# Moving a graph layer's last combination and normalisation out of a stage of its own into the slices' stage, group by group, with the second layer's sums stored to memory at eviction

## The reference

```python
xn = layernorm(x)
enc = h = xn
for l in range(2):                           # two graph attention layers, 8 heads of 64
    q, k, v = h @ Wq[l] + bq[l], h @ Wk[l] + bk[l], h @ Wv[l] + bv[l]
    a = sum(q[dst] * k[src]) / 8             # per edge and head
    e = exp(a - segment_max(a, dst)[dst])
    agg = segment_sum(e / (segment_sum(e, dst)[dst] + 1e-16) * v[src], dst)
    h = agg + (h @ Ws[l] + bs[l]) + enc
y = layernorm(h) * ln_g + ln_b               # this is the last combination
gnn = layernorm(relu(y @ W1 + b1) @ W2 + b2 + y) * ln_g + ln_b + enc
mid = xn @ W_in + b_in                       # the mixer, 8 heads of 64, 32 slices each
q, k, v = softmax(mid @ Wq, over slices), softmax(mid @ Wk, over nodes), mid @ Wv
mix = (q @ (k.T @ v)) @ W_out + b_out
x = x + gnn + mix
out = x + ffn(layernorm(x))                  # ternary weights
```

## Time and profile before

| | us |
|---|---|
| median of 3 runs (3349.22 to 3351.88) | 3349.69 |
| the profiled execution, by its own clock | 3346.05 |
| its span, first to last instruction | 3344.3 |
| PE / DVE / POOL / ACT busy | 2558.1 / 2347.1 / 1708.9 / 1239.1 |
| last eviction of the second layer's sums begins | 2348.76 |
| first transfer of the slices' stage | 2431.69 |
| first transfer of `node_mlp` | 2610.76 |

### The profile page before, as it was taken

How to read it: one execution, slowest core, us unless ns; L and a number is a source line. 1 busy time by engine, 2 the same in 40 slices (tenths; PEclk the granted TensorE clock), 3 DMA queues, 4 the chain that set the end, 5 groups by cost and what they waited for, 6 DMA issues and landing times. The chain is left out here.

```text
span 3344.3 us, 46214 instructions
## 1 busy us (share of the span) xinstructions
PE 2558.1 (76%) x10373; PEld 1750.8 (52%) x10373; DVE 2347.1 (70%) x4332; ACT 1239.1 (37%) x6570; POOL 1708.9 (51%) x1618
## 2 busy tenths in 40 slices
PE   2888866664988869996666668878077799869998
PEld 1766522222765547872222256655056576657776
DVE  5777687778977767767777798777834346476665
ACT  0344378776000011007777700000233232155554
POOL 0101377777777751117777777777400235344444
PEclk8999998988899999998888879999588899989999
DMA  1544577776777775437777767777130323261111
GB/s 41 182 151 163 175 237 236 239 237 195 204 219 226 228 224 161 133 122 240 236 235 239 229 188 224 223 226 221 55 101 13 126 101 114 73 201 38 38 38 37
DMA packets 228144, 549.19 MB, mean 164 GB/s; under 512 B 32920, under 2 KB 50946, under 8 KB 227918
## 3 DMA queue, kind: packets, MB, share of 16 engines
q0 software_dynamic: 106240, 348.21, 35.4%
q1 hardware_dynamic: 110158, 177.31, 15.8%
q10 hardware_dynamic: 11520, 20.98, 1.8%
HBM read 471.88 MB, written 74.49 MB: 163 GB/s over the span
## 5 line engine op out<-in xcount | busy, mean ns | idle before, releaser
L1189 POOL DMA_INDIRECT edge_ring<-v_rows,edges_src x664 | 655.3, 987 | 202.3 <-issue 160.9
L1352 PE MATMUL edge_psQ<-layer_q_space,layer_y_space 128*128 x1992 | 553.2, 426 | 268.1 <-DVE layer_y_space L1220 266.7
L1189 POOL DMA_INDIRECT edge_ring<-k_rows,edges_src x664 | 628.3, 946 | 252.1 <-issue 141.9
L1389 PE MATMUL edge_psA<-layer_q_space,edge_hot 128*128 128x256 f32 (+1 forms) x2656 | 652.6, 398 | 130.9 <-DVE edge_hot L1284 82.8
L1308 ACT ACTIVATE layer_y_space<-layer_y_space 128x64 f32<-128x64 f32 x2656 | 637.2, 241 | 234.3 <-DVE layer_y_space L1220 233.2
L1389 PEld LDWEIGHTS edge_psA<-layer_q_space,edge_hot 128*128 128x128 f32 x2656 | 491.2, 193 | 292.0 <-issue 224.8
L1295 DVE TENSOR_TENSOR layer_q_space<-edge_ring,edge_psQ 128x512 f32<-128x512 f32 x664 | 456.7, 688 | 149.9 <-DMA edge_ring<-v_rows,edges_src 144.4
L1220 DVE TENSOR_TENSOR layer_y_space<-edge_psQ,edge_ring 128x512 f32<-128x512 f32 x664 | 433.8, 685 | 177.9 <-DMA edge_ring<-k_rows,edges_src 165.0
L1352 PEld LDWEIGHTS edge_psQ<-layer_q_space,layer_y_space 128*128 128x128 bf16 x1992 | 211.0, 106 | 610.4 <-issue 512.5
L103 PE MATMUL proj_psP<-proj_w,proj_xT 128*128 128x512 f32 x1920 | 480.4, 409 | 43.9 <-DVE proj_enc L867 32.3
L1308 ACT ACTIVATION_READ_ACCUMULATOR layer_y_space<-layer_y_space 128x1 f32 x2656 | 494.9, 186 | 0.0
(11 more groups left out here) (287 smaller groups left out, 3047.3 us busy)
## 6 DMA issues: line engine op xcount, KB each, us to landing
layer_y_space<-local_rows SPq DMA_DIRECT2D x82, 256.0 KB, 4.5
edge_ring<-k_rows,edges_src POOLq DMA_INDIRECT x664, 3.9
edge_ring<-v_rows,edges_src POOLq DMA_INDIRECT x664, 3.7
base_rows<-proj_enc SPq DMA_DIRECT2D x40, 256.0 KB, 2.0
k_rows<-proj_out ACTq DMA_DIRECT2D x40, 256.0 KB, 3.1
v_rows<-proj_out ACTq DMA_DIRECT2D x40, 256.0 KB, 4.2
ffn_downT<-down_rows SPq DMA_DIRECT2D x11, 512.0 KB, 9.6
agg_rows<-layer_y_space SPq DMA_DIRECT2D x20, 260.0 KB, 3.9
```

The lines of the kernel that those rows point to most:

```text
L1189: pool.indirect_dma_start(ring[:, n % NB, :], None, k_dram if n < USED else v_dram, bass.IndirectOffsetOnAxis(ap=T["src"][:, s:s + 1], axis=0)
L1352: last = pe.matmul(psQ[i][:], hotT[j % 2][:, i * P:(i + 1) * P], one(qp[:, k, bass.ds(tiles[i], 1), :]), start=(k == 0), stop=(k == 2))
L1389: last = pe.matmul(psA[:, bass.ds(d % 2, 1), e, 0:hi - lo].rearrange("p o w -> p (o w)"), hot[:, s % R, :], wv[:, s % R, lo:hi], start=Fal ...
```

## The change

The second layer's sums are stored to `agg_rows` at eviction, as the first layer's are, with four places in SBUF; base isn't loaded there any more. `combine` is gone. `project_slices` becomes `combine_and_project_slices`: for each group SP loads four tiles of sums and of base, VectorE scales and adds one tile behind each running maximum of k, takes the statistics between the subtraction and the sum of q's softmax, and computes the shifts behind it. ScalarE takes the root and writes the normalised rows behind the exponential. GpSimd does `ln_g` and `ln_b` for all 20 tiles. The loops over groups on SP, ACT and VectorE are written out; PE's list is as it was.

The diff, cut to what the text speaks of:

```diff
         B, V, R, NB = 4, 2, 8, 28
-        leaves = layer < LAYERS - 1
-        AB = 4 if leaves else NT
+        AB = 4
         BATCHES = USED // B
...
-                for t in range(NT):
-                    if leaves:
-                        sp.wait_ge(kept, 2 * t + 2)
-                        sp.dma_start(agg_dram[t * P:(t + 1) * P, :], agg[:, t % AB, :]).then_inc(agg_out[t % AB], 16)
-                    else:
-                        if t:
-                            sp.wait_ge(weighted, t * U)
-                        sp.dma_start(x[:, t, :], base_dram[t * P:(t + 1) * P, :]).then_inc(base_in, 16)
-                if leaves:
-                    for b in range(AB):
-                        sp.wait_ge(agg_out[b], 16 * (NT // AB))
-                else:
-                    sp.wait_ge(base_in, 16 * NT)
+                for d in range(NT):
+                    sp.wait_ge(kept, 2 * d + 2)
+                    sp.dma_start(agg_dram[d * P:(d + 1) * P, :], agg[:, d % AB, :]).then_inc(agg_out[d % AB], 16)
+                for b in range(AB):
+                    sp.wait_ge(agg_out[b], 16 * (NT // AB))
...
-                    if leaves and d >= AB:
+                    if d >= AB:
...
-def combine(nc, a, T, layer, agg, x, out_dram):
...
-def project_slices(nc, a, T, xn_dram, qT, folded):
+def combine_and_project_slices(nc, a, T, xn_dram, agg_dram, base_dram, y_dram, qT, folded):
...
+        agg = m.sb("agg", [P, GN, AW])
+        row = m.sb("row", [P, 2, GN, C])
+        den = m.sb("den", [P, GN, H])
+        gb = m.sb("gb", [P, 2, C])
...
+                ln.set_eps(pool)
+                pool.wait_ge(gb_in, 32)
+                for i in range(NT):
+                    at = row[:, i // GN % 2, i % GN, :]
+                    pool.wait_ge(row_normed, i + 1)
+                    pool.tensor_tensor(at, at, gb[:, 0], ALU.mult).then_inc(row_scaled, 1)
+                    pool.wait_ge(row_scaled, i + 1)
+                    pool.tensor_tensor(at, at, gb[:, 1], ALU.add).then_inc(row_done, 1)
...
+                def load_rows(g):
+                    if g:
+                        sp.wait_ge(combined, g * GN)
+                    sp.dma_start(agg[:], rows_of(agg_dram, g)).then_inc(agg_in, 16)
+                    if g >= 2:
+                        sp.wait_ge(row_out[g % 2], 16)
+                        if g >= 4:
+                            sp.wait_ge(row_out[g % 2], 32)
+                    sp.dma_start(row[:, g % 2], rows_of(base_dram, g)).then_inc(row_in[g % 2], 16)
+                def store_rows(g):
+                    sp.wait_ge(row_done, (g + 1) * GN)
+                    sp.dma_start(rows_of(y_dram, g), row[:, g % 2]).then_inc(row_out[g % 2], 16)
...
-                def group(g, end):
-                    if not end:
+                load_rows(0)
+                sp.dma_start(gb[:, 0], a["L0_gnn_ln_g"].partition_broadcast(P)).then_inc(gb_in, 16)
+                sp.dma_start(gb[:, 1], a["L0_gnn_ln_b"].partition_broadcast(P)).then_inc(gb_in, 16)
+                for g in range(GROUPS):
+                    if g < GROUPS - 1:
                         sp.wait_ge(s["turned"], g * GN + GN)
                         load(g + 1)
-                turns_ahead(sp, GROUPS, group)
+                    if g:
+                        store_rows(g - 1)
+                    if g < GROUPS - 1:
+                        load_rows(g + 1)
+                store_rows(GROUPS - 1)
+                for b in range(2):
+                    sp.wait_ge(row_out[b], 16 * len(range(b, GROUPS, 2)))
...
-                turns_ahead(act, GROUPS, group)
+                    ln.root(act, g)
+                    act.wait_ge(row_shifted, g + 1)
+                    for n in range(GN):
+                        at = row[:, g % 2, n, :]
+                        act.activation(at, at, ACT.Identity, bias=shift[:, g % 2, n:n + 1], scale=ln.rstd[:, n:n + 1]
+                                       ).then_inc(row_normed, 1)
+                for g in range(GROUPS):
+                    group(g, g == GROUPS - 1)
...
+                weigh = Chain(vec, weighing)
+                def weights(g):
+                    vec.wait_ge(agg_in, g * 16 + 16)
+                    weigh.then(vec.tensor_scalar(den[:], agg[:, :, C:AW], 1e-16, None, ALU.add))
+                    weigh.wait()
+                    weigh.then(vec.reciprocal(den[:], den[:]))
+                    vec.wait_ge(row_in[g % 2], g // 2 * 16 + 16)
+                    weigh.wait()
+                def combine(g, n):
+                    at = agg[:, n, 0:C].rearrange("p (h d) -> p h d", h=H)
+                    weigh.then(vec.tensor_tensor(at, at, den[:, n].unsqueeze(2).to_broadcast([P, H, D]), ALU.mult))
+                    weigh.wait()
+                    vec.tensor_tensor(row[:, g % 2, n, :], row[:, g % 2, n, :], agg[:, n, 0:C], ALU.add
+                                      ).then_inc(combined, 1)
+                def statistics(g):
+                    vec.wait_ge(combined, (g + 1) * GN)
+                    if g:
+                        vec.wait_ge(row_normed, g * GN)
+                    ln.stats(vec, lambda n: row[:, g % 2, n, :], g)
+                def shifts(g):
+                    ln.scale(vec, g)
+                    vec.scalar_tensor_tensor(out=shift[:, g % 2, :], in0=ln.mv[:, :, 0], scalar=-1.0, in1=ln.rstd[:],
+                                             op0=ALU.mult, op1=ALU.mult).then_inc(row_shifted, 1)
                 def group(g, end, rows_of_last=P):
                     if not end:
                         low(g + 1)
                     if later(g):
                         take_q(g - 1)
                     c = Chain(vec, s["steps"], g * 3)
+                    weights(g)
                     for n in range(GN):
                         k_top(g, n, P if n < GN - 1 else rows_of_last)
+                        combine(g, n)
                     vec.wait_ge(s["q_in"], g * GN + GN)
                     by_head = q[:].rearrange("p n (h s) -> p (n h) s", s=SL)
                     c.then(vec.tensor_reduce(qsum[:], by_head, AX.X, ALU.max))
                     c.wait()
                     vec.tensor_tensor(by_head, by_head, qsum[:].unsqueeze(2).to_broadcast([P, GN * H, SL]),
                                       ALU.subtract).then_inc(s["shifted"], 1)
+                    statistics(g)
                     vec.wait_ge(s["exped"], g + 1)
                     c.then(vec.tensor_reduce(qsum[:], by_head, AX.X, ALU.add))
                     c.wait()
@@ -2082,10 +2065,9 @@
                     c.wait()
                     vec.tensor_tensor(by_head, by_head, qsum[:].unsqueeze(2).to_broadcast([P, GN * H, SL]),
                                       ALU.mult).then_inc(s["normed"], 1)
-                group(0, False)
-                with vec.Fori(1, GROUPS - 1) as g:
-                    group(g, False)
-                group(GROUPS - 1, True, LAST)
+                    shifts(g)
+                for g in range(GROUPS):
+                    group(g, g == GROUPS - 1, P if g < GROUPS - 1 else LAST)
```

More of the change, by code:

```diff
@@ L1873, in project_slices, with rows_of @@
         s = {n: m.sem(n) for n in names}
+        agg = m.sb("agg", [P, GN, AW])
+        row = m.sb("row", [P, 2, GN, C])
+        den = m.sb("den", [P, GN, H])
+        gb = m.sb("gb", [P, 2, C])
+        shift = m.sb("shift", [P, 2, GN])
+        ln = LayerNorm(nc, m, GN)
+        row_in = [m.sem(f"row_in{b}") for b in range(2)]
+        row_out = [m.sem(f"row_out{b}") for b in range(2)]
+        gb_in, agg_in, weighing, combined, row_shifted, row_normed, row_scaled, row_done = (
+            m.sem(n) for n in ("gb_in", "agg_in", "weighing", "combined", "row_shifted", "row_normed", "row_scaled",
+                               "row_done"))
+        def rows_of(dram, g):
+            return dram[g * NODES:(g + 1) * NODES, :].rearrange("(t p) c -> p t c", p=P)
         W2 = 2 * SL
```

92 lines of the change are left out of this document (6 added, 86 removed).

## The result

Before took 3350.78 us (median of 4 runs beside it, 3349.22 to 3354.10), the changed kernel 3326.31 (4 runs, 3324.80 to 3327.44): ratio 0.9925, 95% interval 0.9908 to 0.9943. That is 24.5 us less (the interval allows 19 to 31); 28.8 less, 3321, was forecast. The profiled spans are 3344.3 and 3324.0, 20.3 apart.

What follows compares the result with a forecast made beforehand. PE was taken to bound the slice groups, VectorE the serial combination before them. The terms -78.9 + 38.4 + 7.4 + 3.3 + 1.0 = -28.8 us took 3349.7 to 3321 us, range 3308 to 3335.

Steps and rivals of the forecast that it cites:

- the stall: At four seams between slice groups, ScalarE's first `mid` and PE with it start 9.6 us later: 38.4 us.
- the clock: After each of four seams PE's idle time costs one cold restart of 1.9 us: 7.4 us.
- the tail: Behind the last group: division 3.3 us later, plus 1 us for two small matrices waiting on GpSimd.
- The stage removed: Between the second layer's last eviction and the slices: first transfer comes 78.9 us earlier, 77 to 81.
- The stores: At the second layer's evictions: twenty stores of sums replace twenty loads of base, taken as costing nothing.
- The forecast's signs: Expected trace marks: ScalarE idle 2 to 3 us before the rows, PE idle over 9 us four times, 36 us groups.
- Rival A: At the seams PE's clock holds across the idle time: 3313 us, chance 0.16.
- B: In the slice groups the combination's work hides in full: 3275 us, chance 0.03.
- D: Within groups PE isn't granted full clock again after a seam: 20 us a group more, 3401 us, chance 0.05.
- C: GpSimd and VectorE hinder each other at the seams, or x loads come late: 3330 to 3333 us, chance 0.14.

Runs made afterwards that it cites:

- the run without the combination: The kernel before with its last combination left out, the next stage reading base instead of the normalised rows, so part of the computation is missing: 3270.22 us, ratio 0.9767.
- VectorE's order alone: The changed kernel with only VectorE's list reordered: fourth tile combined behind the subtraction, reciprocal and shift ahead of the sum; 3315.59 us, ratio 0.9888.

## Why the prediction was right

The direction and the mechanism held, and the range held the time. The size held with some luck: the stall came 1.8 us under its price, the clock nearly 5 and the tail 1.8 over theirs. Together these make 24.0 us less for the stages that the change touches, for the 28.8 that was forecast. By its steps:

- **The stage removed**, -78.9: the trace gives -78.9 behind the last eviction, and the run without the combination 78.0.
- **The stores**, 0: the run of their own can't tell 0 from 5 us by its times, and its weighting takes 0.7 us longer.
- **The stall**, 9.6 a seam: the first `mid` was 9.14 later, so 36.6 for 38.4. The rows came a little sooner (K+10.11 for K+10.46). The root was no part of it, as said: the rows waited for the shift. But it was done at K+8.72 and not K+7.5, since its table load began only behind the wait for the statistics (2401.67). The runs with the rows moved show that it was the list's order that turned 2.93 us of activations into 9.
- **The clock**, 7.4, was mis-sized. The blocks behind the four stalls cost 2.55, 2.41, 1.68 and 2.55, together 9.2, and the second dip inside two groups (1.97 us transposes and what follows) about 4 more; before had one such dip itself, so the net is near 12. The run with a busy PE shows the first part. Nearly all of it is block 2, which took 5.49, 5.47, 4.74 and 5.49 us for 3.06; block 3 took at most 3.12 for 2.96. I had priced a restart by one row, the first block of the stage, and that block takes 4.34 to 5.49 us in the twelve traces, so one execution was too few. The second dip wasn't in the sum at all. The Trainium skill's "HAM oscillation — how this bites in real kernels" (in "TensorE: Matmul & The Clock Gate") gives an estimate of 0.8 a seam, 26.7 us in 32 dips; here it was 1.7 to 2.6 for the pair alone, so the mechanism agrees and its figure is too low for this kernel.
- **The tail**, 3.3 + 1: 6.1. The division gave 3.0 and the two small matrices beside GpSimd 0.8 (1.25 for 0.48). The rest is PE again, which the forecast left out: products of k and v 20.61 for 19.90 (granted clock 0.85 for 0.88), and the last eight matmuls 5.22 for 3.70 (0.71 for 1.00). The longer wait ahead of the tail doesn't explain the latter: the run with the rows behind the high parts waits 14.10 us there and takes 3.70. Five of the twelve traces have these matmuls slow, and why stays open.
- **The forecast's signs**: ScalarE was idle for 1.89 us ahead of the table load and 1.40 ahead of the rows, not 2 to 3 at once. The groups took 37.9, 39.2, 35.6 and 31.8 us for the 36 of the forecast, the last one shorter as before.
- **Rival A** (the clock holds) is refuted by the windows, **B** (all hidden) by the gaps of 9.3, **D** by the clock's return to 1.00 inside each group. **C** was absent here (low parts 687 ns, no wait for x), but it is real: it came up as soon as the groups were shorter.
- 3.7 us between the spans lie ahead of the stage and behind it. They are in no term of the forecast, and traces of one code differ by more there.

## What to carry to other kernels

Idle time summed over a stage doesn't tell what can be hidden in it: put the work where each in-order queue has its gaps, behind the instruction that the bounding engine waits for next. The same row activations took the kernel to 3326 us ahead of `mid`, to 3299 behind the blocks, to 3300 behind the high parts and, spread over the gaps with VectorE's and the last group's part fitted to them, to 3282. When PE stalls, count both the stall and the slow instructions after it; and a repaired stall uncovers the next collision, so look again after each step.

## What was not expected of the hardware

- A wait of 1.40 us ahead of the transposes of q occurs in every group but the last. In some it is followed by a granted clock of 0.62 and doubled times (1.97 for 1.09), in others not, and before had it once too. None of the three was slow with PE busy in the stall, but none was either in the run with VectorE's order alone, which kept stalls of 7.2 to 8.5 us; with the rows behind `mid` all three were. What decides it wasn't found.
- GpSimd and VectorE slow each other where VectorE's operation has both inputs in SBUF: its 128x512 addition went from 0.69 to 1.66 us, its 128x1024 division of the softmax from 1.22 to between 1.72 and 2.03, GpSimd's operations from 1.28 up to 2.14. VectorE's low parts, with one input in PSUM, stayed at 0.69 beside GpSimd.
